# Blocks turned in place and moved forward, the multiply by dt moved forward, and a new order of TensorE's work in each unit of a Mamba-2 style mixer kernel

## The reference

```python
proj = x @ in_proj_w.T                       # gate 8192 | hBC 8192 + 2*1024 | dt 128
hBC = silu(causal_conv4(hBC) + conv_b)       # -> hs, B (8 groups x 128), C (8 groups x 128)
xch = hs * dt                                # 128 heads of 64, 4 chunks of 128 tokens
Y_diag  = (C @ B.T * L) @ xch                # inside a chunk; L = exp of differences of sums
states  = B.T @ (decay * xch)                # per chunk, then carried over the chunks
Y_off   = C @ prev_state * exp(A_cum)
y = (Y_diag + Y_off + hs * D) * silu(gate)
out = (group_rms_norm(y) * norm_w) @ out_proj_w.T
```

## Time and profile before

| | us |
|---|---|
| median of 3 runs | 1695.08 |
| lowest and highest run | 1694.08, 1696.36 |
| the profiled execution, its own time | 1687.36 |
| its span in the trace | 1685.6 |
| PE busy in it | 1570.0 (93%) |
| DVE busy | 1376.5 (82%) |
| ACT busy | 1149.9 (68%) |
| POOL busy | 758.2 (45%) |
| mean granted clock of PE | 0.984 |

### The profile page before, as it was taken

How to read it: one execution, slowest core, us unless ns; L and a number is a source line. 1 busy time by engine, 2 the same in 40 slices (tenths; PEclk the granted TensorE clock), 3 DMA queues, 4 the chain that set the end, 5 groups by cost and what they waited for, 6 DMA issues and landing times.

```text
span 1685.6 us, 26384 instructions
## 1 busy us (share of the span) xinstructions
PE 1570.0 (93%) x9072; PEld 1311.4 (78%) x9072; DVE 1376.5 (82%) x2047; ACT 1149.9 (68%) x2020; POOL 758.2 (45%) x535
## 2 busy tenths in 40 slices
PE   7879999899998999999999999989999899999988
PEld 5667888787887788778887788777788778877767
DVE  7677878887888878887788888788878987888777
ACT  5966667666786677666577667666677767776643
POOL 2244444454445444445345535445444544545440
PEclk9999999999999999999999999999999999999989
DMA  4554434443443344344444344434344334343321
GB/s 150 201 159 129 156 124 134 154 143 108 157 150 127 119 150 149 127 136 129 129 160 138 124 146 136 128 132 156 105 146 160 130 117 158 137 142 126 132 66 51
DMA packets 132278, 228.43 MB, mean 136 GB/s; under 512 B 28080, under 2 KB 76720, under 8 KB 131888
## 3 DMA queue, kind: packets, MB, share of 16 engines
q1 hardware_dynamic: 132144, 226.74, 41.0%
HBM read 187.87 MB, written 38.80 MB: 134 GB/s over the span
## 4 chain that ended last, share of the span: by engine, by line
issue 55%; POOL 36%; PE 7%; ACT 1%; DVE 0%; DMA 0%; SPq 0%; POOLq 0%; ACTq 0%; DVEq 0%
POOL w_low L1505 9%; POOL xdecay L1526 8%; POOL square_sum L1513 8%; POOL y L1519 6%; POOL out_low L1544 5%; PE head_bank L823 0%; PE d_bank L834 0%; DMA alog<-a_log 0%; PE head_bank L298 0%; PE g_bank L814 0%; PE g_bank L884 0%; PE d_bank L903 0%; PE g_bank L816 0%; PE head_bank L903 0%; PE d_bank L904 0%
## 5 line engine op out<-in xcount | busy, mean ns | idle before, releaser
L1526 POOL TENSOR_TENSOR xdecay<-xdt,tables 128x384 f32<-128x384 f32 x128 | 165.7, 1314 | 478.5 <-DVE xdt L1332 468.4
L1054 ACT ACTIVATE scores<-scores,tables 128x128 f32<-128x128 f32 x1024 | 312.0, 389 | 0.0
L1519 POOL TENSOR_TENSOR y<-y,gate 128x512 f32<-128x512 f32 x128 | 179.5, 1423 | 272.0 <-DVE y L1303 272.0
L1234 DVE SCALAR_TENSOR_TENSOR hs<-x_bank,cols,hs 128x1022 f32<-128x1022 f32 x189 | 241.6, 1278 | 29.9 <-ACT hs L1067 25.3
L814 PE MATMUL g_bank<-x_high,w_high 128*128 128x512 f32 x624 | 251.0, 402 | 0.0
L816 PE MATMUL g_bank<-x_high,w_low 128*128 128x512 f32 x624 | 243.4, 390 | 0.0
L815 PE MATMUL g_bank<-x_low,w_high 128*128 128x512 f32 x624 | 243.4, 390 | 0.0
L1505 POOL TENSOR_TENSOR w_low<-raw,w_high 128x512 fp32r<-128x512 f32 x139 | 184.9, 1330 | 102.6 <-ACT w_high L1044 102.5
L1067 ACT ACTIVATE hs<-x_bank,cols 128x1024 f32<-128x1024 f32 x63 | 75.7, 1201 | 215.8 <-PE x_bank L816 186.0
L823 PE MATMUL head_bank<-xdecay,b_tok 128*128 128x128 f32 x768 | 120.4, 308 | 90.8 <-POOL xdecay L1526 83.8
L814 PE MATMUL x_bank<-x_high,w_high 128*128 128x512 f32 x504 | 196.4, 390 | 1.8 <-issue 1.8
(11 more groups left out here) (213 smaller groups left out, 3457.6 us busy)
## 6 DMA issues: line engine op xcount, KB each, us to landing
scores<-sums_dram SPq DMA_DIRECT2D x128, 512.0 KB, 4.9
raw<-w_in SPq DMA_DIRECT2D x144, 256.0 KB, 2.7
blocks_dram<-hs SPq DMA_DIRECT2D x63, 512.0 KB, 2.6
quads<-blocks_dram SPq DMA_DIRECT2D x252, 128.0 KB, 3.0
grown_rows<-grown_dram SPq DMA_DIRECT2D x256, 96.0 KB, 2.8
out_raw<-w_out SPq DMA_DIRECT2D x64, 256.0 KB, 3.3
mixed<-x SPq DMA_DIRECT2D x8, 256.0 KB, 4.6
out<-mixed SPq DMA_DIRECT2D x8, 256.0 KB, 2.0
```

Of the source, the lines that this page charges most:

```text
L1054: op = s.activation(at, at, ACT.Relu, bias=col[:, r, c:c + 1], scale=-1.0)
L1234: v.scalar_tensor_tensor(out=hs[:, q % 2, :, i:], in0=x_bank[:, :, 0:SEQ - i], scalar=cols[:, q, TAPS - 1 - i:TAPS - i], in1=hs[:, q % 2, ...
L1519: pool.tensor_tensor(y[:, b], y[:, b], gate[:, q % 2, b], ALU.mult).then_inc(y_ready, 1)
L1526: pool.tensor_tensor(xdecay[:, b], xdt[:, b, 0:LATER], col.unsqueeze(3).to_broadcast([P, LATER, PAIR, HEAD_DIM]), ALU.mult)\
```

## The change

`turn_blocks` writes into `quads` in place of hs, the store reads `quads`, and the loads write `quads` again. So the wait for the skip goes, in its place stands the multiply by dt of the unit before, and ACT's `tap0` no longer waits for the store. DVE turns the blocks right behind the taps, ahead of carried_state. SP loads the quads right behind the store, ahead of the grown rows. DVE does both scores, to_heads, the taps of B or C, and then adds tiles 2 and 3; tiles 0 and 1 are added between skip and carry_part. PE's round becomes: tiles 2 and 3 of the round before, x, gate, states, diagonal, tiles 0 and 1, carry, and the extras of the round. The last unit keeps its order.

```diff
-        def blocks_of(k):
-
-            return hs[:, (k - 1) % 2].rearrange("p b n -> p (b n)")
+        blocks = quads[:].rearrange("p a b c i -> p (a b c i)")
@@ store_blocks, load_quads (SP)
-                sp.dma_start(blocks_dram, blocks_of(k)).then_inc(blocks_stored, 16)
+                sp.dma_start(blocks_dram, blocks).then_inc(blocks_stored, 16)
             def load_quads(k):
                 sp.wait_ge(blocks_stored, 16 * k)
-                sp.wait_ge(xdt_ready, PAIR * k)
@@ SP's round
                         store_blocks(ahead[2])
+                        load_quads(ahead[2])
                         for b in range(BATCH):
                             load_grown(ahead[2], b)
-                        load_quads(ahead[2])
@@ PE's round: states and diagonal from here to behind the gate
-                    if j == 0:
-                        pe.wait_ge(b_tok_ready, g + 1)
-                    for b in range(BATCH):
-                        states(k, b)
-                    for b in range(BATCH):
-                        reached(pe, added, emptied(k - 1, 2 + b))
-                        diagonal(k, s, b)
                     if ahead:
                         pe.wait_ge(gate_ready, BATCH * (k + 1))
...
                             project(ahead[0], x_at + 1, b, g_bank[:, b])
                     if j == 0:
-                        pe.wait_ge(c_ready, g + 1)
+                        pe.wait_ge(b_tok_ready, g + 1)
+                    for b in range(BATCH):
+                        states(k, b)
+                    for b in range(BATCH):
+                        reached(pe, added, emptied(k - 1, 2 + b))
+                        diagonal(k, s, b)
                     if not ahead:
                         pe.wait_ge(added, emptied(k - 1, 0))
                         out_product(j, 0)
-                    for b in range(BATCH):
-                        carry(k, b)
+                        for b in range(BATCH):
+                            carry(k, b)
@@ behind output tiles 0 and 1
+                    if j == 0:
+                        pe.wait_ge(c_ready, g + 1)
+                    if ahead:
+                        for b in range(BATCH):
+                            carry(k, b)
@@ tap0 (ACT)
-                reached(s, blocks_stored, 16 * (k - 1))
@@ turn_blocks (DVE)
-                v.wait_ge(skip_added, k)
-                v.transpose(blocks_of(k).rearrange("p (m n i) -> p n m i", m=QUADS, i=QUAD),
+                reached(v, xdt_ready, PAIR * k)
+                v.transpose(blocks.rearrange("p (m n i) -> p n m i", m=QUADS, i=QUAD),
@@ DVE's round
-                    if k > 2:
-                        add_outs(g, j - 1, (2,))
+                    if last or j not in (5, 6):
+                        for b in range(BATCH):
+                            score(g, j, k, b)
+                    if k > 0:
+                        to_heads(g, j, k)
                     if j in (5, 6) and not last:
                         for i in range(1, TAPS):
                             bc_tap(i, 2 * (g + 1) + j - 5, j - 5)
-                    scores_here = last or j not in (5, 6)
-                    if scores_here:
-                        score(g, j, k, 0)
                     if k > 2:
-                        add_outs(g, j - 1, (3,))
-                    if scores_here:
-                        score(g, j, k, 1)
-                    if k > 0:
-                        to_heads(g, j, k)
+                        add_outs(g, j - 1, (2, 3))
...
+                    if ahead:
+                        turn_blocks(k + 1)
                     for b in range(BATCH):
                         carried_state(*now, b)
                     if ahead:
                         skip(j, k)
-                        turn_blocks(k + 1)
+                        if k > 1:
+                            add_outs(g, j, (0, 1))
+                        else:
+                            dense_of(BATCH + k, x_bank[:, 0])
                         for b in range(BATCH):
                             carry_part(k, b)
...
-                    if k > 1:
                         add_outs(g, j, (0, 1))
-                    else:
-                        dense_of(BATCH + k, x_bank[:, 0])
```

## The result

The changed kernel takes 1770.15 us (median of 4 runs, 1767.83 to 1784.72) against 1695.72 of the kernel before: a ratio of 1.046, 95% interval 1.040 to 1.052. It is 4.6% slower, where 1.1% faster was forecast, and 70 us above the top of the range. The profiled execution took 1784.72 us, the longest of the four and 15 above the median, so sums from its trace come out somewhat large (by 1.8 us in each of the eight groups, if they share it evenly).

A forecast was written before the change was run, and what follows sets the result against it. PE, busy 93% (DVE 82%), was taken to lose 15.6 us a group to waits and their after-effects. Groups -26 and clock +7 sum to -19, so the median goes from 1695 to 1676 us, range 1632 to 1700.

The forecast's parts named there:

- the one on the DMAs: SP's store behind the sums' load starts near 18.2, lands after 2.6; quads there at about 26; cost nothing.
- The cover: Quads there 5 us into the next round, DVE comes to them at 7: 2 us in hand.
- The multiply by dt forward: Ends near 9, POOL's xdecay about 3 later, states begin at 13.6: PE's xdecay wait goes altogether in plain rounds.
- DVE's round: 16.8 us without scores, plus 4.7 for the pair of scores beside POOL's multiply: 21.5, above PE's 21.0.
- Turning in place: Transpose right behind the taps, ahead of carried_state: DVE must sit out ACT's silu, 1.2 us a round.
- The group: Eight rounds sum to 196.0 us, 2.2 less a group; 13 in groups 1 to 6, 14 first, -1 last: 26.
- The clock: Clock fall while PE waits for the squares: 1 us for each of seven groups, +7; bounds 0 and 1.7.
- the slower one, by the clock: Rival: PE's waits in rounds 1 to 3 make the clock fall in each; 1697 to 1728, taken 1710; chance 0.18.
- a sign of being wrong: Listed under "Wrong": DVE idle ahead of to_heads for the quads; no size given.

The follow-up runs named there:

- the last experiment: Changed kernel with store ahead of sums, tiles 0 and 1 behind add_carry, norm steps behind taps, squares' reduction ahead of to_heads in round 1: 1593.27 us, ratio 0.940.

## Why the prediction was wrong

**The step that failed is the one on the DMAs, "I cost this at nothing; that 2 us is the cover".** It had seen that the store would now stand behind the loads of the sums, which wait for the diagonal, and it had put the store's issue near 18.2, 1.5 us behind the transpose's end by its own times (15.4 and 1.25). Two terms of it were mis-sized.

The larger is the landing. It took 2.6 us from a kernel in which the sums were issued 5.8 us ahead of the store (median). In the changed kernel that distance is 2.3 us, and the store needs 5.1 us to the loads behind it; where it was 1.1 us, in rounds 1 and 7, it needed 7.4, where it was 7.9, in round 2, it needed 2.7 (means).

The other is the issue. The median delay, 1.5 us, is as laid out, but it is 4.2 and 3.6 us in rounds 1 and 7, and 4.4 and 5.4 in rounds 4 and 5, where a weight tile that waits for POOL holds the store; the prediction did not name that tile.

The cover itself was well sized. With the store ahead, issued at once or nearly so, the quads land 3.3 us (median) before DVE comes; less the delay of 1.5 us that leaves 1.8, where 2 was forecast. A landing 2.5 us longer is more than that. What the runs showed in place of "nothing" is 104.6 us of DVE's idle, and 92 us with the order on SP mended: 1678, where 1676 was forecast.

*The multiply by dt forward:* right. The wait for xdecay went from 83.8 to 6.8 us.

*DVE's round:* right for the scores. 4.7 was taken for the pair, 4.54 measured, a mean of 2.30 us where "near 2.3" stood. The rule of the Trainium skill, SBUF — State Buffer, section "Who interferes with whom", that the one fully blocks the other, fits the changed kernel's row (4.54) and not the 3.35 of one wait. But the same port was costed at two more places by the durations of before, and these moved: y_low from 1.33 to 1.72 us, 25 us in all, and the norm steps from 1.22 to 1.65, 27 us. Both grow with the POOL instruction that stands beside them (a norm step from 0.75 us beside none to 1.33 before and 1.78 now), and in the round shown the change put w_low and the square there. A part of both goes back with the store ahead (y_low to 1.52 us, a norm step to 1.58), so it comes of the late quads. DVE's busy time rose by 148 us, not "some 100".

*Turning in place:* right, 1.2 us a round for the silu, 73.9 us in 63. That it is on the path was hardly so: covered by other work it gave 7 us, in the one order in which that was tried.

*The group:* it failed by the quads (rounds 0, 2, 5, 6, 7) and in rounds 2 and 3 by the norm steps. Round 4 (26.3 for 26.4) and, with the store first, rounds 4 to 7 (98.0 for 98.5) are as laid out. Besides the quads the forecast missed some in rounds 0 and 1 (47.3 for 46.1, and 45.5 before) and more in rounds 2 and 3 (53.8 for 51.4, and 49.3 before). Counted from tap to tap the first of these falls into round 0, since the first tap of round 1 stands on ACT behind a step that waits for DVE's reduction of the squares, as in the changed kernel's trace:

```profile
720.12 1.21 DVE L1364 TENSOR_REDUCE squares<-g_bank 128x8 f32<-128x1024 f32 x1
...
721.36 0.30 ACT L1121 ACTIVATE g_std<-squares,eps_col 128x8 f32<-128x8 f32 x1 [2.35 <-DVE squares L1364]
721.57 1.19 ACT L1066 ACTIVATE hs<-x_bank,cols 128x1024 f32<-128x1024 f32 x1
```

The reduction ahead of to_heads brought rounds 0 and 1 together down by 3.7 us in the last experiment.

*The clock:* 1 us a group was taken. The trace shows stretches of 1.2 GHz in round 1 and round 2, a mean of 0.953, and with the store first 0.970 at a time in line with the forecast. How much of the 75 us it makes was not measured by itself. PE was busy 33 us longer for the same 9072 matmuls (4 us with the store first), so the clock makes up to some 30 us (an estimate, from those two busy times). It goes with PE's waits: the edit on SP alone takes most of it away.

*The rivals:* the slower one, by the clock, had the sign but not the mechanism, and with 1728 at most not the size. The mechanism that came, DVE idle ahead of to_heads for the quads, stood in the text only as a sign of being wrong. Its price could have been had from the same parts: a store that lands no sooner than the sums ahead of it, which took 4.9 us by the page of before, rather than in 2.6.

## What to carry to other kernels

When a step is moved on one engine, follow the queue that issues DMAs: what waits for that step there, how many bytes it then puts just ahead of a small transfer that is urgent, and how long that transfer takes to land behind them. A landing time read from a trace holds for that distance to the big transfers only. And where a second engine is nearly as busy as the first, look in the trace for those of its operations that take longer beside a third engine's (here DVE's scores, 1.38 to 2.30 us beside POOL's multiply, and the norm steps), and try another place for them before making that engine wait anywhere: the norm steps' place was worth 42 to 46 us here, the scores' 8 to 13.

## What the runs showed that was not expected

A store of 512 KB landed in 2.6 us with 1 MB of loads issued 6 to 20 us ahead, in 3.8 with an eighth of those bytes and a weight tile close ahead, in 5.1 with all of them and the tile close ahead, and the loads behind it waited up to 8.1 us for it. Less work on DVE gave little as long as the quads were late (145 us less for 38 us), yet moving the norm steps, which left the wait for the quads at 95 us, gave 46: it came off rounds 2 and 3, and but for round 2 the quads' loss sat in others. And the two smallest parts, the gate ahead of the states and the store ahead of the sums, gave 5.5% on the kernel before, while the first alone gave 1.2%; the second alone was not run.
